# Second mixture's first half: all turned rows copied by ScalarE, gate logits ahead of the last quarter's v products, no memset behind its sends

## The chip, the cores and the metric

The kernel runs on one core of one Trainium2 chip, as one program. The time is the device time of that core in microseconds (us), from a launch to its end. The five engines are named as in the profile: PE is TensorE (its weight loads are PEld), DVE is VectorE, ACT is ScalarE, POOL is GpSimd, SP is SyncE, which here only issues DMAs. Each engine works through its own list of instructions in order. They meet through semaphores: a wait at the head of an engine's list holds back all that stands behind it.

## The reference

Two decoder layers on `x` of shape (2, 1024, 256), float32, with a layer norm behind each of six blocks. Only the last three matter here:

```python
x = _layernorm(x + _L1_attn_ref(x, ...), axis=-1)    # recurrent mix: k, v, r products, a scan over time
x = _layernorm(x + _L1_xattn_ref(x, ctx_1024, ctx_1024, ...), axis=-1)   # one head over 64 context rows
x = _layernorm(x + _L1_ffn_ref(x, ...), axis=-1)     # 16 experts and two shared ones

# in _L1_attn_ref, xt the normalised rows and x_prev the row before
K = einsum('btc,dc->btd', xt * mk + x_prev * (1.0 - mk), Wk)     # V and R alike, R through a sigmoid
S = scan(state * decay + k_t)
y = einsum('btc,dc->btd', R * ((S * first + K) * V), Wo)

# in _L1_ffn_ref
scores = jax.nn.sigmoid(x @ w_gate.T)                # 16 experts in 4 groups
top_groups = jax.lax.top_k(group_scores, 2)[1]       # two groups, then four experts of theirs
_, idx = jax.lax.top_k(masked, 4)
w = w / (w.sum(-1, keepdims=True) + 1e-06)
routed = einsum('tef,ehf,te->th', silu(x @ w1) * (x @ w3), w2_e, combine)
```

## The kernel before, in words

The 2048 rows are 16 tiles of 128 rows and stay in SBUF. The program is a chain of stages, each a block of its own on all engines: two attentions, the first mixture of experts, then `recurrent_stage` and `moe1_stage`. A stage begins on an engine when all engines have left the one before.

**The recurrent stage** does the recurrent mix and the second cross attention in four quarters of 512 rows. What each engine does, in which order, is one list of steps, `recurrent_plan`. Every engine goes through the whole list and does its part of each step. A step is (name, quarter, part): `k`, `v`, `r` are products of a quarter (two parts of 128 output columns each, L2229), `y` the output product (L2237), `x4` the norm behind it, `tx` turns (transposes) the normed rows, `s` makes the scores, `ta` turns the softmax's exponentials, `o` is the attention's result (L2285) and `x5` the norm behind it. For each norm, DVE takes the moments, POOL makes the reciprocal root in `spread_of` (L1979 to L1985), and DVE (x4) or ACT (x5) applies it.

Into the last quarter's steps the list already puts the first half of the routing for the second mixture, for rows 0 to 1023 (half 0):

- `tg` (L2266): PE turns the finished rows of quarters 0 and 1, four steps of four transposes. The result is copied from PSUM to `xTf`, parts 0 by ACT (L2064), parts 1 by DVE (L2182).
- `lg` (L2275): PE multiplies `xTf` by the gate's 16 columns. It first waits until all four turned parts are copied. ACT puts the exponential into `ex` (L2067).
- `c` parts 0 to 3: DVE picks groups and experts (`choose`, L2399 to L2433).
- `ct` (L2478): PE counts; `lc`: DVE works out each row's place (`locate`, L2441 to L2454), and sets `pos_ready`.
- `sx`: POOL sends rows to their places with `scatter`. One send is an indirect DMA of one tile of 128 rows (L2389); behind it stands `ch.pause`, a memset of 16 columns (L112) with a wait for it.

Half 0 has 8 tiles times 4 choices, 32 sends. Three are issued behind `pos_ready`, ten after step `y` of quarter 3, and the other 19 at the start of the next stage.

**The mixture stage** starts with the same work for half 1 (turn, logits L2823, choose, count, locate) and the shared experts (L2841, L2852). SP waits for all 32 sends of half 0, then loads the first sorted rows from `Xd` into `xin` (L2557). PE turns them (L2862), multiplies them with the experts' weights (L2879, L2891), item after item, 46 or so double tiles in a row. POOL sends half 1 meanwhile, two sends per item, each with its pause. At the end POOL gathers the results (L2601), and DVE adds, weighs and normalises.

PSUM banks of the recurrent stage are in two rings of four, `m` for k, v and r and `a` for the rest; a step waits until its bank's last use is drained.

Of the kernel before, what the change touches and what calls it, by code (L numbers as in the profile page):

```python
# [35 lines left out]
class Scope:  # L36
# [8 lines left out]
    def ps(self, name, shape, dt=F32):  # L45
        return self.stack.enter_context(self.nc.psum_tensor(f"{self.name}_{name}", shape, dt))

    def sem(self, name):
        s = self.stack.enter_context(self.nc.semaphore(f"{self.name}_{name}"))
        self.sems.append(s.num)  # L50
        return s
# [1788 lines left out]
def recurrent_plan():  # L1840


    plan = [("st", 0, 0), ("st", 1, 0), ("xn", 0, 0), ("tn", 0, 0), ("tn", 0, 1), ("df", 0, 0), ("mk", 0, 0), ("mv", 0, 0),
            ("mr", 0, 0), ("xn", 1, 0), ("kt", 0, 0), ("kt", 0, 1), ("km", 0, 0), ("km", 0, 1), ("bq", 0, 0)]
    for q in range(QUARTERS + 2):
        n, p, z = q + 1, q - 1, q - 2
        steps = [("x4", p, 0), ("x4", p, 1), ("k", q, 0), ("k", q, 1), ("x5", z, 0), ("x5", z, 1), ("tx", p, 0), ("tx", p, 1),
                 ("tn", n, 0), ("tn", n, 1), ("v", q, 0), ("v", q, 1), ("df", n, 0), ("s", p, 0), ("mk", n, 0), ("mv", n, 0),
                 ("r", q, 0), ("r", q, 1), ("ta", p, 0), ("dn", p, 0), ("rs", q, 0), ("rs", q, 1), ("st", q + 2, 0),
                 ("mr", n, 0), ("o", p, 0), ("o", p, 1), ("y", q, 0), ("y", q, 1), ("xn", q + 2, 0)]  # L1850
        plan += [x for x in steps if 0 <= x[1] < QUARTERS]

    def put(step, *new):
        at = plan.index(step) + 1
        plan[at:at] = new

    put(("tx", 2, 1), ("tg", 0, 0), ("tg", 0, 1), ("tg", 1, 0), ("tg", 1, 1))
    put(("v", 3, 1), ("lg", 0, 0), ("c", 0, 0), ("c", 0, 1), ("c", 0, 2), ("c", 0, 3))
    put(("r", 3, 0), ("ct", 0, 0))
    put(("r", 3, 1), ("lc", 0, 0), ("sx", 0, 3))  # L1860
    put(("y", 3, 1), ("sx", 3, 13))
    return plan
# [10 lines left out]
def recurrent_stage(nc, a, G, experts1, route):  # L1873
# [46 lines left out]
    R = ps("R", [P, 8, 512])  # L1920
# [4 lines left out]
    free = [sem(f"bank_free{n}") for n in range(8)]  # L1925
# [11 lines left out]
    def filled(eng, step):  # L1937

        bank, n = at[step]
        eng.wait_ge(ready[bank], n)  # L1940
# [18 lines left out]
    with nc.Block() as block:  # L1959

        @block.sync
        def _(sp):
            sp.dma_start(cols[:, :, :], a["rwkv_cols"]).then_inc(cols_in, 16)
            sp.dma_start(w[:, :, :, :], a["rwkv_w"]).then_inc(w_in, 16)
            for to, name in ((wkT, "xk1"), (ctxT, "ctxT"), (wq, "xq1"), (ctx, "ctx")):
                sp.dma_start(to[:, :, :], a[name]).then_inc(x_in, 16)
            sp.dma_start(bk[:, :], a["bk1"]).then_inc(x_in, 16)
            sp.dma_start(bq[:, :], a["bq1"]).then_inc(x_in, 16)
            sp.dma_start(m_i[:, :], a["mask1"].rearrange("b k -> (b k)").partition_broadcast(P)).then_inc(x_in, 16)
            experts1.prefetch(sp, a)  # L1970
# [46 lines left out]
        @block.scalar  # L2017
        def _(act):
            act.wait_ge(cols_in, 16)
            act.activation(decay[:, :], cols[:, 5, :], ACT.Sigmoid)  # L2020
            act.activation(first[:, :], cols[:, 6, :], ACT.Exp).then_inc(consts, 1)
            for what, q, k in PLAN:
                step, p = (what, q, k), q % 2
                if step in at.at:
                    bank, _n = at[step]
                if what == "xn":
                    act.wait_ge(rstd_ready[0], q + 1)
                    if q:
                        filled(act, ("tn", q - 1, 1))
                    for j in range(J):  # L2030
                        act.activation(xn[:, j, :], G.x_sb[:, q * J + j, :], ACT.Identity, bias=shift[0][p][:, j:j + 1],
                                       scale=rstd[0][p][:, j:j + 1]).then_inc(xn_ready, 1)
                if what == "tn":
                    filled(act, step)
                    act.activation(xt[:, k, column(q, 0)], R[:, bank, :], ACT.Identity,
                                   bias=cols[:, 1, k:k + 1], scale=cols[:, 0, k:k + 1]).then_inc(free[bank], 1)
                if what == "r":
                    filled(act, step)
                    if q:
                        act.wait_ge(rw_ready, KD * (q - 1) + k + 1)  # L2040
                    act.activation(sig[:, k, :], R[:, bank, :], ACT.Sigmoid).then_inc(free[bank], 1)
                if what == "kt":
                    filled(act, step)
                    act.activation(kT[:, k, :], R[:, bank, 0:K2], ACT.Identity, bias=bk[:, k:k + 1]).then_inc(free[bank], 1)
                if what == "tx":
                    filled(act, step)
                    if q:
                        filled(act, ("s", q - 1, 0))
                    act.activation(xT[:, 2 * k:2 * k + 2, :, :], R[:, bank, :].rearrange("p (t k c) -> p t k c", t=2, k=KD),
                                   ACT.Copy).then_inc(free[bank], 1)  # L2050
                if what == "s":
                    act.wait_ge(sub_ready, q + 1)
                    if q:
                        act.wait_ge(den_ready, q)
                        filled(act, ("ta", q - 1, 0))
                    act.activation(e[:, :, :], sub[:, :, :], ACT.Exp).then_inc(exp_done, 1)
                if what == "ta":
                    filled(act, step)
                    if q:
                        filled(act, ("o", q - 1, 1))  # L2060
                    act.activation(aT[:, :], R[0:SK, bank, :], ACT.Copy).then_inc(free[bank], 1)
                if what == "tg" and k == 0:
                    filled(act, step)
                    act.activation(route.xTf[:, k, 512 * q:512 * (q + 1)], R[:, bank, :], ACT.Copy).then_inc(free[bank], 1)  # L2064
                if what == "lg":
                    filled(act, step)
                    act.activation(route.ex[:, 0, :], R[:, bank, 0:route.CE], ACT.Exp, scale=-1.0).then_inc(free[bank], 1)  # L2067
                if what == "x5":
                    act.wait_ge(rstd_ready[2], 2 * q + k + 1)
                    for j in (2 * k, 2 * k + 1):  # L2070
                        last = act.activation(G.x_sb[:, q * J + j, :], xr[2][:, j, :], ACT.Identity,
                                              bias=shift[2][p][:, j:j + 1], scale=rstd[2][p][:, j:j + 1])
                    last.then_inc(x5_ready, 1)

        @block.vector
        def _(dve):
            ch = Chain(dve, c_dve)

            def moments(n, p, x_of, js):

                s = [ch.done(dve.bn_stats(st[n][p][:, j, :], x_of(j))) for j in js]
                for m, j in enumerate(js):
                    ch.wait(s[m])
                    last = dve.bn_aggr(mv[n][p][:, j, :], st[n][p][:, j, :])
                last.then_inc(var_ready[n], 1)

            for what, q, k in PLAN:
                step, p = (what, q, k), q % 2
                if step in at.at:
                    bank, _n = at[step]  # L2090
                if what == "st":
                    moments(0, p, lambda j: G.x_sb[:, q * J + j, :], range(J))
                if what in ("mk", "mv", "mr"):
                    n = ("mk", "mv", "mr").index(what)
# [18 lines left out]
                if what == "k" and k == KD - 1:  # L2113
# [10 lines left out]
                    for d in range(KD):  # L2124
                        ch.wait(scans[d])
                        bank = at[("k", q, d)][0]
# [41 lines left out]
                if what == "o":  # L2168
# [8 lines left out]
                    last.then_inc(free[bank], 1)  # L2177
                    drained(dve, step)
                    moments(2, p, lambda j: xr[2][:, j, :], (2 * k, 2 * k + 1))
                if what == "tg" and k == 1:  # L2180
                    filled(dve, step)
                    dve.tensor_copy(route.xTf[:, k, 512 * q:512 * (q + 1)], R[:, bank, :]).then_inc(free[bank], 1)  # L2182
                if what == "c":
                    if k == 0:
                        dve.wait_ge(route.consts, 1)
# [2 lines left out]
                if what == "lc":  # L2188
                    filled(dve, ("ct", 0, 0))
                    bank = at[("ct", 0, 0)][0]  # L2190
# [127 lines left out]
class Route1:  # L2318
# [64 lines left out]
    def scatter(self, pool, ch, G, Xd, n, lo, hi, rest):  # L2383

        pool.wait_ge(G.zeroed, 16)
        pool.wait_ge(self.pos_ready, n + 1)
        for m in range(lo, hi):
            s, r = m // self.W.K, m % self.W.K
            pool.indirect_dma_start(Xd[:, :], bass.IndirectOffsetOnAxis(self.pos[:, n, r, s:s + 1], 0),  # L2389
                                    G.x_sb[:, self.W.TH * n + s, :], None).then_inc(self.scattered[n], 16)  # L2390
            ch.pause(rest)

    def choose(self, dve, ch, n, part):

# [705 lines left out]
```

## Time and profile before

| what | us |
|---|---|
| median of 3 runs | 1311.39 (1308.12 to 1311.88) |
| the profiled execution | 1302.48 |
| its span | 1300.2 |
| PE busy | 1135.8 (87%) |
| DVE busy | 698.4 (54%) |
| ACT busy | 585.8 (45%) |
| POOL busy | 468.5 (36%) |

The profiled execution is a single one, 8.9 us shorter than the median of the runs. Its span leaves out 2.3 us around the program. The busy shares are averages over stages with different limits: the recurrent stage ends and the mixture stage starts at about 1063 us, and the part in question lies between 1010 and 1094 us, where no engine is busy throughout. PE's granted clock is given for each stretch as a share of the full 2.4 GHz; 0.50 is the other level, 1.2 GHz.

### The profile page before, as it was taken

How to read it: one execution, taken by the hardware profiler on the slowest of the kernel's cores; microseconds unless marked ns; L12 is line 12 of the kernel's file. 1: busy time of each engine (PE TensorE's matmuls, PEld its weight loads, DVE VectorE, ACT ScalarE, POOL GpSimd, SP SyncE). 2: the span in 40 equal slices, each digit the busy share in tenths (PEclk: the TensorE clock that was granted, in tenths of full speed). 3: DMA queues.
4: the chain of work that ended last, by engine and by line, in shares of the span. 5: the costliest groups of instructions: out<-in, count | busy, mean ns of one | idle time of the engine just before them, and what ended most of it. 6: DMA issues, size and time to landing. Idle time of an engine off the chain costs nothing. (4 is left out here: it accounts for less than half of the span.)

```text
span 1300.2 us, 23677 instructions
## 1 busy us (share of the span) xinstructions
PE 1135.8 (87%) x7485; PEld 826.0 (64%) x7526; DVE 698.4 (54%) x1886; ACT 585.8 (45%) x1071; POOL 468.5 (36%) x906
## 2 busy tenths in 40 slices
PE   7799898999877876999999999999598757999991
PEld 4344444444344543889999999988455545999961
DVE  4766666766344543622323232338589846555647
ACT  3267677677756643222323232332244222557720
POOL 7445332231422332013323232301323176716456
PEclk9699999999988997999999999999699858999996
DMA  9900200000000006501111111130520014867633
GB/s 349 359 2 9 91 1 1 1 1 1 2 1 1 1 1 216 243 17 34 41 34 41 34 39 36 38 124 19 183 95 1 13 62 140 259 194 237 216 105 122
DMA packets 68128, 109.31 MB, mean 84 GB/s; under 512 B 7346, under 2 KB 54963, under 8 KB 65203
## 3 DMA queue, kind: packets, MB, share of 16 engines
q1 hardware_dynamic: 58130, 80.96, 18.2%
q0 software_dynamic: 9888, 27.01, 6.5%
q8 instruction: 54, 0.88, 0.3%
q14 instruction: 56, 0.45, 0.1%
HBM read 65.61 MB, written 42.34 MB: 83 GB/s over the span
## 5 line engine op out<-in xcount | busy, mean ns | idle before, releaser
L1440 ACT ACTIVATE f_work<-f_bank,f_ub 128x128 f32<-128x128 f32 x312 | 89.0, 368 | 204.3 <-PE f_bank L1762 204.3
L512 ACT ACTIVATE att_PT<-att_RB 128x1024 f32<-128x1024 f32 (+1 forms) x192 | 147.8, 808 | 66.2 <-PE att_RB L651 35.0
L557 DVE CUSTOM_DVE_ANT_0 att_junk<-att_RB,att_causal_q 128x128 f32<-128x128 f32 (+3 forms) x256 | 120.6, 488 | 53.2 <-PE att_RB L633 43.9
L1762 PEld LDWEIGHTS f_bank<-f_work,f_xTf 128*128 128x128 f32 x1248 | 145.3, 192 | 3.9 <-DVE f_work L1562 2.0
L1762 PE MATMUL f_bank<-f_work,f_xTf 128*128 128x128 f32 x1248 | 145.9, 275 | 1.5 <-DVE f_work L1562 1.5
L1771 PE MATMUL f_bank<-wd_down,f_work 128*128 x624 | 141.2, 380 | 0.0
L633 PE MATMUL att_RB<-att_kT,att_qT 96*128 96x512 bf16 (+3 forms) x384 | 120.5, 350 | 20.4 <-DVE att_mx L557 6.8
L1771 PEld LDWEIGHTS f_bank<-wd_down,f_work 128*128 128x128 f32 x624 | 115.7, 190 | 13.9
L1391 POOL DMA_INDIRECT Yd<-f_work,f_inv x39 | 38.5, 987 | 196.3 <-DVE f_work L1581 196.3
L1571 DVE COPY f_xTf<-wu_up 128x1024 f32 x78 | 54.1, 695 | 102.6 <-PE f_bank L1762 94.9
L633 PEld LDWEIGHTS att_RB<-att_kT,att_qT 96*128 96x128 bf16 x384 | 34.4, 100 | 110.3 <-issue 39.1
L561 DVE TENSOR_REDUCE att_mx<-att_RB 128x1 f32<-128x512 f32 x128 | 88.1, 689 | 21.4 <-PE att_RB L633 21.1
L648 PE MATMUL att_RB<-att_qT,att_kT 128*128 128x512 bf16 (+3 forms) x353 | 94.6, 327 | 2.6 <-ACT att_PT L512 1.5
L2879 PEld LDWEIGHTS f_bank<-f_xT,f_staged 128*128 128x128 f32 x752 | 91.9, 193 | 2.6 <-DVE f_xT L2701 0.3
L2879 PE MATMUL f_bank<-f_xT,f_staged 128*128 128x128 f32 x752 | 92.3, 277 | 0.0
L2601 POOL DMA_INDIRECT f_ga<-Yd,r_pos x64 | 63.0, 984 | 72.3 <-DMA Yd<-f_yo 53.9
L2389 POOL DMA_INDIRECT Xd<-g_x,r_pos x64 | 64.2, 1003 | 52.7 <-DVE r_pos L2454 27.8
L663 PE MATMUL att_OT<-att_PT,att_vst 128*32 128x512 f32 (+3 forms) x768 | 82.5, 501 | 0.0
L1386 POOL DMA_INDIRECT f_work<-Xd,f_inv x39 | 50.4, 1293 | 77.8 <-PE f_bank L1737 66.2
L1581 DVE TENSOR_TENSOR f_work<-f_bank,f_db 128x256 f32<-128x256 f32 x39 | 16.6, 425 | 108.3 <-PE f_bank L1771 108.3
L384 POOL TENSOR_SCALAR att_negm<-att_rowmax 128x8 f32<-128x8 f32 x32 | 7.8, 245 | 179.6 <-DVE att_rowmax L565 179.6
L1726 PE MATMUL f_bank<-f_xTf,wu_up 128*128 128x256 f32 x256 | 57.1, 381 | 1.5 <-ACT f_work L1430 1.5
(462 smaller groups left out, 2150.9 us busy)
## 6 DMA issues: line engine op xcount, KB each, us to landing
Xd<-g_zero SPq DMA_DIRECT2D x1, 12032.0 KB, 40.7
f_xin<-Xd SPq DMA_DIRECT2D x47, 256.0 KB, 3.8
Yd<-f_yo SPq DMA_DIRECT2D x47, 256.0 KB, 2.8
wu_up<-up_w SPq DMA_DIRECT2D x9, 1024.0 KB, 9.0
wd_down<-down_w SPq DMA_DIRECT2D x9, 1024.0 KB, 18.4
w_all<-w SPq DMA_DIRECT2D x6, 768.0 KB, 10.6
wu_up<-Yd SPq DMA_DIRECT2D x16, 256.0 KB, 5.7
w_all<-w SPq DMA_DIRECT2D x1, 2304.0 KB, 17.2
```

What stands on the lines that cost most here:

```text
L512: act.activation(buf[:, :, 0:w], ST[:, 2 * (k % 2):2 * (k % 2) + 2, 0:w], ACT.Exp, scale=float(HD) ** -0.5).then_inc(exp_done, 1)
L557: dve.tensor_tensor_reduce(junk[:, k % RING, 0:w], RB[:, bank, 0:w], G.causal_q[:, 512 - w:512], 1.0, LOWEST, ALU.add, ALU.max, to).then_i ...
L561: dve.tensor_reduce(to, RB[:, bank, :], AX_X, ALU.max).then_inc(bank_free[bank], 1)
L633: pe.matmul(RB[:, bank, 0:w], qT[1 - p][0:MROW, r, t * P:(t + 1) * P], kT[1 - p][0:MROW, 512 * c:512 * c + w], start=True, stop=True).then ...
L648: mm = pe.matmul(to[:, 0:512 - off], kT[p][:, kt * P:(kt + 1) * P], qT[p][:, r, 512 * c + off:512 * c + 512], start=True, stop=not diag)
L663: mm = pe.matmul(OT[32 * r:32 * r + 32, off:512], vst[p][:, kt, :], PT[k % 4][:, h, 0:512 - off], start=(kt == 0), stop=(kt == 4 * c + 3))
L1440: last = act.activation(hT[:, u % 2, m, :], bank[:, UB + m // 4, (m % 4) * P:(m % 4 + 1) * P], ACT.Gelu, bias=ub[:, ds(e, 1), m])
L1762: mm = pe.matmul(bank[:, UB + n, P * m:P * (m + 1)], staged_up[:, kk, at:at + P], xT[:, u % 2, kk, :], start=(kk == 0), stop=(kk == KD - 1))
L1771: mm = pe.matmul(bank[:, YB + u % 2, 0:D], hT[:, u % 2, m, :], W.down[:, ds(e, 1), m, :].rearrange("p o c -> p (o c)"), start=(m == 0), st ...
L2389: pool.indirect_dma_start(Xd[:, :], bass.IndirectOffsetOnAxis(self.pos[:, n, r, s:s + 1], 0), G.x_sb[:, self.W.TH * n + s, :], None).then_ ...
L2601: pool.indirect_dma_start(ga[:, s, r, :], None, Yd[0:P * R * (n + 1), :], bass.IndirectOffsetOnAxis(pos[:, n, r, s:s + 1], 0)).then_inc(ga ...
L2879: mm = pe.matmul(bank[:, UB + p, P * at:P * (at + 1)], staged_up[:, q % 3, i, kk, F * part:F * (part + 1)], xT[:, p, i, kk, :], start=(kk ...
```

## The change

Three things are edited. The copies of all four turned parts are ACT's, DVE's two are gone. In the list of steps `lg` stands directly behind the last `tg`, ahead of the v products of quarter 3, where it stood behind them; DVE's `c` steps keep their place behind `v`. And for half 0 the pause behind each send is gone, in both stages; half 1 keeps it.

```diff
@@ recurrent_plan
-    put(("tx", 2, 1), ("tg", 0, 0), ("tg", 0, 1), ("tg", 1, 0), ("tg", 1, 1))
-    put(("v", 3, 1), ("lg", 0, 0), ("c", 0, 0), ("c", 0, 1), ("c", 0, 2), ("c", 0, 3))
+    put(("tx", 2, 1), ("tg", 0, 0), ("tg", 0, 1), ("tg", 1, 0), ("tg", 1, 1), ("lg", 0, 0))
+    put(("v", 3, 1), ("c", 0, 0), ("c", 0, 1), ("c", 0, 2), ("c", 0, 3))
@@ recurrent_stage, scalar
-                if what == "tg" and k == 0:
+                if what == "tg":
                     filled(act, step)
                     act.activation(route.xTf[:, k, 512 * q:512 * (q + 1)], R[:, bank, :], ACT.Copy).then_inc(free[bank], 1)
@@ recurrent_stage, vector
-                if what == "tg" and k == 1:
-                    filled(dve, step)
-                    dve.tensor_copy(route.xTf[:, k, 512 * q:512 * (q + 1)], R[:, bank, :]).then_inc(free[bank], 1)
@@ Route1.scatter
-            ch.pause(rest)
+            if n:
+                ch.pause(rest)
```

PE's list in the recurrent stage before, from the turned rows (`g_x` against the identity) to the counting of the chosen experts (`r_hot`); `rx_xm,rx_w` are the v and r products, `w_gate,r_xTf` the logits, `rx_km,rx_xT` the scores:

```order
L2266 MATMUL rx_R<-g_ident_f,g_x 128x128 x16
L2229 MATMUL rx_R<-rx_xm,rx_w 128x512 x4
L2275 MATMUL rx_R<-w_gate,r_xTf 128x16 x16
L2256 MATMUL rx_R<-rx_km,rx_xT 128x64 x8
L2229 MATMUL rx_R<-rx_xm,rx_w 128x512 x2
L2478 MATMUL rx_R<-r_hot,r_upper 128x128 x4
```

The same place of PE's list now (line numbers are three or two lower):

```order
L2263 MATMUL rx_R<-g_ident_f,g_x 128x128 x16
L2272 MATMUL rx_R<-w_gate,r_xTf 128x16 x16
L2226 MATMUL rx_R<-rx_xm,rx_w 128x512 x4
L2253 MATMUL rx_R<-rx_km,rx_xT 128x64 x8
L2226 MATMUL rx_R<-rx_xm,rx_w 128x512 x2
L2476 MATMUL rx_R<-r_hot,r_upper 128x128 x4
```

The 16 logit products and the four v products have changed places; nothing else on PE moved.

DVE's list at the same place before, from the scan of the last quarter to the first steps of the choice of experts:

```order
L2119 SCALAR_TENSOR_TENSOR rx_state<-rx_decay,rx_state,rx_R 128x512 x2
L2127 SCALAR_TENSOR_TENSOR rx_rw<-rx_state,rx_first,rx_R 128x512 x2
L2182 COPY r_xTf<-rx_R 128x512 x2
L2132 TENSOR_TENSOR rx_rw<-rx_rw,rx_R 128x512 x2
L2399 TENSOR_SCALAR r_ex<-r_ex 128x128
L2400 RECIPROCAL r_sg<-r_ex 128x128
```

DVE's list there now:

```order
L2119 SCALAR_TENSOR_TENSOR rx_state<-rx_decay,rx_state,rx_R 128x512 x2
L2127 SCALAR_TENSOR_TENSOR rx_rw<-rx_state,rx_first,rx_R 128x512 x2
L2132 TENSOR_TENSOR rx_rw<-rx_rw,rx_R 128x512 x2
L2397 TENSOR_SCALAR r_ex<-r_ex 128x128
L2398 RECIPROCAL r_sg<-r_ex 128x128
```

The two copies are gone. The two multiplications by v (`rx_rw<-rx_rw,rx_R`) still stand ahead of the choice (`r_ex`, `r_sg`).

POOL's list at the start of the mixture stage now, with the 19 sends left of half 0, the first one of half 1 in the same row, and then half 1's sends with their memsets:

```order
L2577 MEMSET f_half 128x4
L2386 DMA Xd<-g_x,r_pos 12032x256 x20
L112 MEMSET r_rest 128x16
L2386 DMA Xd<-g_x,r_pos 12032x256
L112 MEMSET r_rest 128x16
```

Before, each of the 20 sends had a memset row of its own behind it.

## Rows read from the trace of the kernel before

**Rows 1.** Chain that ended last, in order of time: start us, us, what.

```profile
1063.86 1.07 POOL Xd L2389
...
1089.03 2.45 DMA Xd<-g_x,r_pos
1091.49 2.79 DMA f_xin<-Xd
```

**Rows 2.** Waits of PE, 1000 to 1180: total us, times, longest.

```profile
PE f_bank L2862 <- DMA f_xin<-Xd: 7.7, 1, 7.7
```

**Rows 3.** Timeline of PE, 1010 to 1044: start us, us, [idle before].

```profile
1010.06 1.91 PE L2266 MATMUL rx_R<-g_ident_f,g_x 128*128 128x128 f32 x16
1011.81 3.60 PE L2229 MATMUL rx_R<-rx_xm,rx_w 128*128 128x512 f32 x8
1015.25 3.64 PE L2275 MATMUL rx_R<-w_gate,r_xTf 128*128 128x16 f32 x32
1018.74 3.29 PE L2256 MATMUL rx_R<-rx_km,rx_xT 128*128 128x64 f32 x16
1021.82 3.73 PE L2229 MATMUL rx_R<-rx_xm,rx_w 128*128 128x512 f32 x4
1027.87 0.38 PE L2478 MATMUL rx_R<-r_hot,r_upper 128*128 128x128 bf16 x4 [2.32 <-DVE r_hot L2433]
1028.32 1.94 PE L2229 MATMUL rx_R<-rx_xm,rx_w 128*128 128x512 f32 x4
1035.48 3.69 PE L2237 MATMUL rx_R<-rx_w,rx_rw 128*128 128x256 f32 x16 [1.08 <-DVE rx_rw L2136]
1043.77 2.17 PE L2244 MATMUL rx_R<-g_ident_f,g_x 128*128 128x128 f32 x8 [4.60 <-DVE g_x L2148]
```

**Rows 4.** Timeline of ACT at the turned rows.

```profile
1010.76 0.59 ACT L2064 ACTIVATE r_xTf<-rx_R 128x512 f32<-128x512 f32 x1
1011.57 0.60 ACT L2064 ACTIVATE r_xTf<-rx_R 128x512 f32<-128x512 f32 x1 [0.22 <-PE rx_R L2266]
```

**Rows 5.** Timeline of DVE, 1015 to 1059.

```profile
1015.45 0.69 DVE L2132 TENSOR_TENSOR rx_rw<-rx_rw,rx_R 128x512 f32<-128x512 f32 x1 [0.54 <-PE rx_R L2229]
1019.31 0.23 DVE L2399 TENSOR_SCALAR r_ex<-r_ex 128x128 f32<-128x128 f32 x1 [3.17 <-ACT r_ex L2067]
...
1040.39 0.66 DVE L2140 SCALAR_TENSOR_TENSOR rx_xr<-g_x,rx_R 128x512 f32<-128x512 f32 x1
...
1041.75 0.30 DVE L2084 BATCH_NORM_AGGREGATE rx_mv<-rx_st 128x2 f32<-128x6 f32 x2
...
1058.50 0.30 DVE L2084 BATCH_NORM_AGGREGATE rx_mv<-rx_st 128x2 f32<-128x6 f32 x2
```

**Rows 6.** Timeline of POOL, 1042 to 1060, at its norms.

```profile
1042.83 0.22 POOL L1979 TENSOR_SCALAR rx_rstd<-rx_mv 128x2 f32<-128x2 f32 x1
...
1059.26 0.23 POOL L1979 TENSOR_SCALAR rx_rstd<-rx_mv 128x2 f32<-128x2 f32 x1
```

**Rows 7.** Groups of POOL, 1063 to 1091: xcount, busy us, mean ns, idle before.

```profile
L2389 POOL DMA_INDIRECT Xd<-g_x,r_pos x19 | 18.9, 995 | 5.6 <-POOL r_rest L112 5.0 <-issue 0.7
L112 POOL MEMSET r_rest<- 128x16 f32 x19 | 2.4, 125 | 0.0
```

**Rows 8.** Groups of POOL, 1260 to 1291, gathers without a memset between them.

```profile
L2601 POOL DMA_INDIRECT f_ga<-Yd,r_pos x21 | 21.4, 1019 | 6.1 <-issue 6.1
```

**Rows 9.** Stretches: busy us of PE, PEld, DVE, ACT, POOL, then granted clock.

```profile
1019.00:1022.00 3.00, 3.00 (x17) 3.00 (x17) 2.49 (x10) 0.20 (x1) 0.00 (x0) 0.52 0.00 0
1022.00:1025.00 3.00, 3.00 (x5) 0.94 (x4) 2.72 (x17) 0.00 (x0) 0.00 (x0) 0.50 0.01 3
1043.50:1048.00 4.50, 4.23 (x19) 3.83 (x20) 0.92 (x3) 2.48 (x3) 3.75 (x7) 0.50 0.16 58
1067.00:1070.00 3.00, 2.33 (x21) 2.36 (x22) 2.63 (x5) 0.00 (x0) 2.44 (x5) 1.00 0.29 102
1070.50:1077.00 6.50, 6.50 (x15) 3.72 (x15) 5.56 (x20) 4.36 (x6) 5.11 (x11) 0.50 0.26 91
```

## The prediction, written before the result was known

> **What bounds the kernel now.** I read the chain that ended last first. It goes back only to 1063 us, to the start of the mixture stage, and its first members are POOL's sends of half 0: the first of 19 starts at 1063.86, the last at 1089.03, its rows land 2.45 us later, SP's load of the sorted rows takes 2.79 us, and only then, at 1094.42, PE turns them [rows 1]. The waits of PE say the same from the other side: 7.7 us for that load, the longest single wait of the stretch [rows 2]. From there PE works without a gap to about 1237, so what reaches 1094 earlier or later moves the end by as much, up to 7.7 us earlier. Ahead of 1063 the chain gives nothing, because the stage boundary cuts it, so I follow the recurrent stage by the engines' timelines. Its end is made by the last norm: POOL starts it at 1059.26, ACT applies it, and the next stage's POOL and PE start behind that. Back from there the links are score and attention of quarter 3, the turn at 1043.77, for which PE waited 4.60 us, the norm before it, the output product at 1035.48, and DVE, which from 1019.31 works nearly without pause through choice, place and norms [rows 3, 5, 6]. What started DVE at 1019.31 was the logits' exponential, 3.17 us of wait. So a shift of that start moves the whole tail of the stage, and the sends with it.
>
> **Logits ahead of v, and the copies.** Before, PE went from the turned rows straight into v at 1011.81, since v waits for nothing here [rows 3]. Now the logits are next, and they need all four copies. ACT began its two at 1010.76 and 1011.57, 0.6 us each, the second at once when PE had it ready [rows 4]; PE ends the fourth group of transposes near 1011.97 (1010.06 + 1.91). Four copies in a row on ACT, about half a us apart, end near 1012.8, and with about 0.15 us for the semaphore PE begins the logits at 1013.0. That is 1.2 us in which PE stands. The logits themselves take 3.44 + 0.05 us as before (1015.25 to 1018.74), v 3.60, so v's last product is done at 1013.0 + 3.5 + 3.6 = 1020.1. The exponential is ready at about 1016.9, 2.4 us earlier than before, but this is worth nothing: in DVE's order both multiplications by v stand ahead of the choice. Before, the second of them ran at 1015.45 and the choice waited for the exponential; now the choice waits for v, plus a multiplication of 0.69 (0.62 until the next may start) [rows 5]. It starts at 20.1 + 0.04 + 0.62 = 1020.75, against 1019.31: **1.4 us later**. The bounds are 0.9 (ACT's copies keep up with PE, 0.5 us less) and 1.9 (each of the added copies costs its full 0.6). The two copies taken from DVE gain nothing: they ran at a time when DVE would next have waited for v anyway, and DVE had 3.17 us to spare. Scores and r behind v on PE are pushed back too, and what hides them is DVE, which takes 8.4 us from the start of the choice to its last step while PE needs 6.
>
> **PE's clock under the v products.** This is the larger term. The granted clock was full up to 1019, and 0.52 and 0.50 in the two stretches from there, right behind the 32 logit products of 16 columns; it was back after the r product [rows 3, 9]. The same happened in the mixture stage: 1.00 from 1067 to 1070 while its logits began, 0.50 from 1070.5 to 1077 [rows 9]. Both times the fall to 1.2 GHz came during or just behind logits, and the lower level lasted about 6.7 us. Before, this fell on scores and one part of r, which DVE hides. Now it falls on v, for which DVE waits. Price from rows: four product records took 3.73 us at the lower level and 1.94 at the higher, in a row of eight 1.80 [rows 3]; so each record costs 0.48 more, and all eight 3.9. If the fall comes at the end of the logits, 5.5 to 6.5 us of lower level lie over v, six or seven records, 2.9 to 3.4 us. If it comes later, or the level is back earlier, half of it. I take **+3.0**, with 0 and 4.5 (all of v and the last of the logits) as ends.
>
> The Trainium skill, page "TensorE: Matmul & The Clock Gate", section "Part 1: The HAM clock gate", says that the gate goes by how busy the array has been of late and runs freely, not reset by the kernel. By that, the place of the fall differs from one execution to the next, and an execution in which it misses v would come out 3.0 us earlier than my sum. The trace agrees as far as it goes: two levels only, and two falls at logits, at different distances from their start.
>
> **POOL in the recurrent stage.** Three sends lose their pauses. A pause is 0.125 us of memset and 0.28 of wait (5.0 over 18), 0.405 together [rows 7]. Without one there is still a gap: 21 gathers without memsets had 6.1 us of "issue" before them, 0.30 each [rows 8]. So a send gains 0.105, not 0.405, except the last of a run, behind which a norm follows at once. Two gaps and one end: about 0.4 us. POOL came to the norm of `y` at 1042.83, when DVE's moments had been there since 1042.05 (1041.75 + 0.30) [rows 5, 6]; it was late by 0.8, so the 0.4 counts in full: **-0.4**. The ten sends behind it gain 1.1 us on POOL; the last norm started at 1059.26, DVE's moments were ready at 1058.80 (1058.50 + 0.30), and with POOL free it starts some 0.08 behind them: **-0.4**, and the other 0.7 is lost in waiting for DVE.
>
> **The 19 sends of the mixture stage.** They are on the chain. Removed: 18 pauses of 0.405, 7.3 us. Added: 18 gaps of 0.30, 5.4 us. **-1.9 us.** The ends: -7.3 if the sends close up entirely; and nothing, or half a us lost, if a send without pause is longer, as the gathers' 1019 ns stand to the sends' 995 [rows 7, 8]. I stay by the 0.30 because it is the gap of the same kind of instruction on the same engine. What is late next is not near: PE would wait until 1094.42 - 7.7 = 1086.7. Half 1's own sends keep their pauses and are paced by the items.
>
> **Sum.** 1.4 + 3.0 - 0.4 - 0.4 - 1.9 = +1.7 us. On the profiled execution, 1302.48, this gives 1304.2; its span goes from 1300.2 to 1301.9. The median of the runs is 8.9 us above that execution; the difference carries over, so the predicted time is 1311.4 + 1.7 = **1313.1**. What a measurement here can tell from no change is about 0.3%, 3.9 us, so this is "the same", on the slow side.
>
> **The rivals.** (a) PE's clock stays high through v, or the lower level is over before: 1.4 - 0.4 - 0.4 - 1.9 = -1.3, 1310.1. For it: the stretch of logits is only 3.5 us, and in this trace the level outlived it. Against: the 1 us of standing ahead of the logits is new. (b) Slower: the clock falls a second time, in the wait before the counting. With the choice 4.4 us later, counting starts near 1032.3 (1027.87 + 4.4), while scores and r, at the full level, end near 1026.7; PE stands over 5 us where it stood 2.32. Before, it stood 4.60 ahead of the turn at 1043.77, and the level was 0.50 behind it [rows 3, 9]. Then r's second part costs 1.8 more, the attention's output 1.8 by the same ratio, and y, 3.69 us, at least its first half, 1.8: 5.4. About 1.2 is hidden, since y was done at 1039.17 and DVE took its second half at 1040.39, and 0.8 by POOL's lateness and 0.4 by the rest: +3.0 above my sum, 1316.1. It decides from the point where PE's standing passes that of 1043.77. (c) Pauses are worth their full length: the 19 sends gain 7.3 instead of 1.9, sum 1.7 - 5.4 = -3.7, 1307.7. For it: the queue might accept the next send at once. Against: 0.30 stands before every gather of rows 8. (d) Nothing that is listed: a loss elsewhere, or the measurement.
>
> **How the numbers follow.** Forecast 0.40, (a) 0.27, (b) 0.20, (c) 0.05, rest 0.08. The likeliest is 1313.1, its own range 1311 to 1315 by the ends of the clock term. For 8 in 10 the range takes in (a) and (b) with the spread of the medians, 1308.1 to 1311.9 before: 1306 to 1317.5. Faster by over 0.3%, below 1307.5: most of (c), a little of (a) by spread, 0.10. Slower by over 0.3%, above 1315.3: 0.6 of (b), a little of the forecast, 0.18. The rest, 0.72, within.
>
> **What would show it.** In the changed trace: PE starts the logits 1 us or so behind the last transposes, at 1013; `r_ex` on ACT is early by over 2 us, and DVE's step on it is later than before, behind a wait for PE's v and not for ACT. The eight v records take 5 to 7 us together and the granted clock there is 0.5; if they take 3.6, (a) holds. Counting starts after 1029. The gaps between POOL's sends are "issue", 0.30. The last norm starts some 0.1 us behind DVE's moments. From the first of 19 sends to the last takes 23.3 us instead of 25.2. Wrong would be: gaps near zero, a choice that starts before 1019.3, or a wait of PE for the load that isn't the last gate before the experts.

## The result and the profile after

The changed kernel took 1319.53 us (median of 5 runs, 1318.57 to 1323.02), the kernel before beside it 1311.88 (1308.12 to 1312.32): ratio 1.006, 95% interval 1.0036 to 1.0083, 7.65 us slower. The prediction was 1313.1, in a range that ended at 1317.5. The profiled execution took 1318.57 us; its span, 1316.6, stands against 1300.2 of before. The profile's page begins so (busy us, share of the span, instructions):

```profile
span 1316.6 us, 23643 instructions
PE 1143.1 (87%) x7485; PEld 828.8 (63%) x7526; DVE 697.9 (53%) x1884; ACT 585.8 (44%) x1073; POOL 466.5 (35%) x874
```

The busy times of DVE, ACT and POOL are those of before within 2 us. PE's is 7.3 us longer, nearly all of it in four rows at its lower clock: the logits 0.7, v 2.8, the second part of r 1.4, and 1.9 in the shared experts' down products further down. The other 9 us of the longer span are standing time. First the recurrent stage, PE's timeline (start, us, engine, line, operation, count, idle before and its releaser); it answers to [rows 3]:

```profile
1009.10 1.91 PE L2263 MATMUL rx_R<-g_ident_f,g_x 128*128 128x128 f32 x16
1012.00 4.36 PE L2272 MATMUL rx_R<-w_gate,r_xTf 128*128 128x16 f32 x32 [0.99 <-ACT r_xTf L2064]
1016.19 6.41 PE L2226 MATMUL rx_R<-rx_xm,rx_w 128*128 128x512 f32 x8
1031.80 0.59 PE L2476 MATMUL rx_R<-r_hot,r_upper 128*128 128x128 bf16 x4 [5.69 <-DVE r_hot L2431]
1032.61 3.30 PE L2226 MATMUL rx_R<-rx_xm,rx_w 128*128 128x512 f32 x4
1039.44 3.69 PE L2234 MATMUL rx_R<-rx_w,rx_rw 128*128 128x256 f32 x16 [0.32 <-DVE rx_rw L2136]
1047.33 2.17 PE L2241 MATMUL rx_R<-g_ident_f,g_x 128*128 128x128 f32 x8 [4.20 <-DVE g_x L2148]
```

DVE there, with its two v multiplications and the choice behind them ([rows 5]), and the granted clock by stretches (seventh column from the stretch's length on; 1.00 is 2.4 GHz, 0.50 is 1.2; [rows 9]):

```profile
1019.99 0.69 DVE L2132 TENSOR_TENSOR rx_rw<-rx_rw,rx_R 128x512 f32<-128x512 f32 x1 [7.85 <-PE rx_R L2226]
1022.64 0.69 DVE L2132 TENSOR_TENSOR rx_rw<-rx_rw,rx_R 128x512 f32<-128x512 f32 x1 [1.97 <-PE rx_R L2226]
1023.25 0.22 DVE L2397 TENSOR_SCALAR r_ex<-r_ex 128x128 f32<-128x128 f32 x1
```

```profile
1012.00:1014.80 2.80, 2.80 (x26) 2.80 (x26) 0.14 (x1) 1.15 (x1) 0.00 (x0) 1.00 0.03 6
1014.90:1021.90 7.00, 7.00 (x15) 3.77 (x15) 0.69 (x1) 0.28 (x1) 0.00 (x0) 0.51 0.00 0
1028.90:1035.20 6.30, 3.40 (x11) 1.95 (x12) 5.92 (x34) 2.24 (x3) 0.00 (x0) 0.50 0.01 1
1035.40:1043.00 7.60, 6.47 (x30) 4.74 (x28) 7.43 (x23) 1.07 (x2) 3.95 (x6) 1.00 0.13 46
```

PE was at 2.4 GHz through the first logits, fell to 1.2 in their last part and stayed there through the v products, which took 6.41 us instead of 3.60. The choice of experts started 14.15 us behind the turns (1023.25 - 1009.10) instead of 9.25. "Behind the turns" counts from PE's first `tg` transpose here and below. The clock fell again in PE's wait before the counts, as rival (b) said, but was back before `y`, which took its 3.69 us as before. POOL's sends and the last norm ([rows 6, 7]):

```profile
1050.28 0.96 POOL L2386 DMA_INDIRECT Xd<-g_x,r_pos  x1 [0.30 <-issue]
1062.45 0.23 POOL L1979 TENSOR_SCALAR rx_rstd<-rx_mv 128x2 f32<-128x2 f32 x1 [0.29 <-DVE rx_mv L2084]
1067.04 1.07 POOL L2386 DMA_INDIRECT Xd<-g_x,r_pos  x1 [0.65 <-issue]
1090.76 0.96 POOL L2386 DMA_INDIRECT Xd<-g_x,r_pos  x1 [0.30 <-issue]
```

The gap is the forecast 0.30 of "issue", and the row of 19 takes 23.7 us from first to last start, where it took 25.17 [rows 1]. So far this trace explains about +4 - 1.5 us. What comes next was in no step of mine. The chain that ended last, then PE and DVE in the mixture stage ([rows 1, 2]):

```profile
1084.70 8.23 another core or an unknown queue
1092.97 5.59 PE f_bank L2850 x16
```

```profile
1092.97 5.59 PE L2850 MATMUL f_bank<-w_all,f_hs 128*128 128x256 f32 x16 [8.28 <-remote]
1098.85 1.04 PE L2860 MATMUL f_bank<-g_ident_f,f_xin 128*128 128x128 f32 x8
1105.57 3.78 PE L2877 MATMUL f_bank<-f_xT,f_staged 128*128 128x128 f32 x16 [5.68 <-DVE f_xT L2699]
```

```profile
1084.42 0.18 DVE L2426 FIND_INDEX8 r_ix<-r_top,r_ma 128x8 uint32<-128x16 f32 x1 [0.71 <-issue]
1086.55 0.18 DVE L2426 FIND_INDEX8 r_ix<-r_top,r_ma 128x8 uint32<-128x16 f32 x1 [1.17 <-issue]
1092.93 0.18 DVE L2429 CAST r_ixf<-r_ix 128x32 f32<-128x32 uint32 x1 [4.26 <-remote]
```

Before the shared experts' down products PE stood 8.28 us, and DVE stood too, in the middle of eight like instructions that wait for nothing, and once more for 4.26 us behind them, while POOL's sends ran on at 1.27 us each. "Remote" means that no recorded signal explains the release. Indeed records are missing: of the 4817 semaphore updates that this trace's instructions make, 174 have none; in the trace of before all 4849 are there. Of the landings of DMAs it has 3691 records, where another trace of the same program (e8 below) has 6022. Every instruction of DVE and POOL is recorded.

The shared experts' end was now PE's last gate: it turned the first gathered rows at 1098.85 with no wait for their load, which was 7.7 us in [rows 2]. The prediction had named such a thing as a sign of being wrong. Half 1's counts stood behind the down products on PE, so DVE, which works out half 1's places ahead of its copy of the turned rows, came late as well, and PE stood another 5.68 us before the first product with an expert's weights:

```profile
1099.05 0.42 DVE L2439 TENSOR_TENSOR_SCAN r_incl<-r_keep,f_bank 128x128 f32<-128x128 f32 x1 [4.20 <-PE f_bank L2476]
1104.84 1.28 DVE L2699 COPY f_xT<-f_bank 128x512 f32<-128x512 f32 x2
```

### The profile page after: what moved, and what is told of

Its sections match the earlier page's. It is cut to its first block and busy times, and to the rows that moved or that the text cites. A ratio compares the mean times of both kernels' runs of the same rounds, so it can differ in the third digit from the quotient of the medians.

```text
span 1316.6 us, 23643 instructions
## 1 busy us (share of the span) xinstructions
PE 1143.1 (87%) x7485; PEld 828.8 (63%) x7526; DVE 697.9 (53%) x1884; ACT 585.8 (44%) x1073; POOL 466.5 (35%) x874
```

## Experiments

Eighteen runs on five chips, each timed over 5 rounds against the kernel before on the same chip; results are ratios to it, with a 95% interval. The chips fall into two kinds. On chips 3 and 0 no trace lost an update, and the kernel before took 1302.2 us. On chips 2, 7 and 15 every trace (one a run) lost 155 to 183 updates of instructions, and it took 1312.1, 1308.6 and 1308.2. The run of record is of the second kind (1311.9 for the kernel before, 174 updates lost in the changed one's trace), the profile of before, at 1302.48, of the first. Below, "last send to turn" is the time from the start of the last of the 19 sends to PE's first turn of gathered rows (5.39 before, from 1089.03 to 1094.42), "loop" from there to the last down product of an expert (147.4 before), and the recurrent stage ends with ACT's last norm (51.8 behind the turns before).

### The parts of the change (chip 3)

e1, the order and the copies with all pauses kept:

```diff
-            if n:
-                ch.pause(rest)
+            ch.pause(rest)
```

> The changed order of steps and ACT's copies alone, every send with its pause. Theory A (order): v behind the logits, on a PE that has fallen to 1.2 GHz, makes DVE start the choice 3 to 5 us later than before; all of it reaches the end, as before the pauses gave back only 0.8 in this stage: 4 to 5 us above the kernel before, and no wait of several us in the shared experts of the mixture stage. Rival B (pauses): the whole loss of the changed kernel (7.7 us) comes from sends without pause; then this run is within 2 us of the kernel before. Rival C: the 8 us wait in the mixture stage comes from the new order, then it is here again.

Measured 1.0036 (1.0024 to 1.0047), +4.7 us. PE in its trace, logits and v:

```profile
1011.03 4.40 PE L2272 MATMUL rx_R<-w_gate,r_xTf 128*128 128x16 f32 x32 [0.99 <-ACT r_xTf L2064]
1015.26 6.37 PE L2226 MATMUL rx_R<-rx_xm,rx_w 128*128 128x512 f32 x8
```

No stand-still followed, and the stage's end moved by 4.96 us. That is theory A. So order plus clock is +4.4 forecast, +4.7 measured.

e2, the kernel before without half 0's pauses and nothing else:

```diff
-            ch.pause(rest)
+            if n:
+                ch.pause(rest)
```

> The pauses of half 0 alone are gone, order and copies as before. By my sum the sends would give 0.8 + 1.9 = 2.7 us. Theory B: sends without a pause between them hold up the other engines: several of them stop together for up to 8 us at the end of the 19 sends, and the run is 3 to 8 us slower than the kernel before in spite of the gain on POOL. Rival: that wait was the bad luck of one execution; then this run is 1 to 3 us faster than the kernel before.

Measured 0.9974 (0.9962 to 0.9986), -3.4 us by the ratio, -1.8 by the medians, around my -2.7. e3 and e4 are the kernel before and the changed kernel, unchanged.

> The kernel before, unchanged, for a second profile and for the spread: the same time within 0.3%. If waits of several engines together come by chance, this profile should have some as well, as its runs are 9 us above its first profile; if they come only with sends without pause, it has none and PE goes from one item to the next in 3.09 us throughout.

> The changed kernel, unchanged, for a second profile: 6 to 9 us above the kernel before. If the wait of 8.3 us ahead of the shared experts' second product belongs to the change, it is here again at the same place; if it is chance, it is elsewhere or gone. The gate's place should differ: with PE at 2.4 GHz through v the choice starts 1.4 us later than before, at 1.2 GHz 3 to 5.

e3: 0.9995 (0.9982 to 1.0007). e4: 1.0011 (0.9999 to 1.0023), +1.4 to +1.7 us: the prediction's sum, and not the 6 to 9 that I expected of e4 from the run of record. In e4's trace:

```profile
1008.07 3.72 PE L2272 MATMUL rx_R<-w_gate,r_xTf 128*128 128x16 f32 x32 [0.99 <-ACT r_xTf L2064]
1011.63 5.38 PE L2226 MATMUL rx_R<-rx_xm,rx_w 128*128 128x512 f32 x8
```

The same program spent 5.38 us on v here and 6.41 in the run of record, because the fall came and went at another place. That agrees with the rule of the Trainium skill, page "TensorE: Matmul & The Clock Gate", section "Part 1: The HAM clock gate", that the gate runs freely and is not reset by a kernel's start.

### Cures for the clock and the order (chip 0)

e5, the changed kernel with DVE's two last v multiplications behind the choice:

```diff
-                if what == "v":
-                    filled(dve, step)
-                    ...
+                if what == "v" and q < QUARTERS - 1:
+                    times_v(q, k)
@@ c, k == 3
+                        times_v(3, 0)
+                        times_v(3, 1)
```

> The changed kernel, with DVE's two multiplications by v of the last quarter moved behind the choice of experts. If the cost of the new order is that the choice waits for v (my step), the choice now starts about 2.5 us earlier than in the kernel before instead of 3 to 5 later; the two multiplications, 1.3 us, come onto DVE's path behind it, and the pauses' gain stays: 2 to 5 us faster than the kernel before. Rival: PE, not DVE, holds the stage at this place (counting stands behind scores and r on PE, which still ends near 1026); then most of it is lost and the run is within 1 us of the kernel before.

Measured 0.9986 (0.9977 to 0.9995), 3.9 us under the changed kernel (e8, on the same chip) and 1.8 under the kernel before, between the forecast's 2 to 5 and the rival's 1. The choice began 7.76 us behind the turns, but the clock then fell under `y`:

```profile
1025.02 0.39 PE L2483 MATMUL rx_R<-r_hot,r_upper 128*128 128x128 bf16 x4
1030.30 3.13 PE L2289 MATMUL rx_R<-rx_ctx,rx_aT 64*128 64x256 f32 x8 [2.27 <-ACT rx_aT L2061]
1033.36 5.88 PE L2241 MATMUL rx_R<-rx_w,rx_rw 128*128 128x256 f32 x16
```

e6, the changed kernel with logits four times as wide (ACT first copies the gate's 16 columns four times, and reads one of the four results for its exponential):

```diff
-                            mm = pe.matmul(R[:, bank, experts1.E * s:experts1.E * (s + 1)],
-                                           route.xTf[:, kk, s * P:(s + 1) * P], experts1.gate[:, kk, :],
+                            mm = pe.matmul(R[:, bank, 64 * s:64 * (s + 1)],
+                                           route.xTf[:, kk, s * P:(s + 1) * P], route.gate4[:, kk, :],
```

> The changed kernel, its 32 logit products 64 columns wide instead of 16 (the gate four times side by side, of which one copy is read), as many products at the same pace. If the fall of PE's clock under v is owed to what the array does in the logits, it stays at 2.4 GHz through v more often: v takes 3.6 us instead of 5.4 to 6.4, the choice starts 1.4 us later than in the kernel before, and the run is 1.5 to 3 us below the changed kernel. Rival: the standing still ahead of the logits makes the fall, or 64 columns are no different; then v is as slow as in the changed kernel and the time the same within 0.1%.

Measured 0.9986 (0.9978 to 0.9995), 3.7 us under the changed kernel for more columns of work:

```profile
1010.10 3.76 PE L2279 MATMUL rx_R<-r_gate,r_xTf 128*128 128x64 f32 x32 [0.99 <-ACT r_xTf L2069]
1013.69 3.65 PE L2233 MATMUL rx_R<-rx_xm,rx_w 128*128 128x512 f32 x8
```

The logits took 3.76 us instead of 4.36, v 3.65 instead of 6.41. The edit leaves the number and the order of PE's products alone, and PE stands the same 0.99 us ahead of the logits, so this standing alone doesn't make the clock fall. In the changed order v took 3.65 us in all four traces with wide logits (e6, e9, e17, e18), and 5.38 to 6.41 in all seven with narrow ones. The choice started 10.79 us behind the turns, 1.55 later than in the kernel before: that is the term of order and copies by itself, and the 3.36 from there to 14.15 is the clock's.

e7, the kernel before with all copies on ACT (`if what == "tg":`, DVE's two removed), and e8, the changed kernel for the third time:

> The kernel before with one edit, all four turned parts copied by ACT, the logits behind v as before and every pause kept. My step says nothing is gained or lost: DVE had 3.17 us of wait there and ACT is idle. Same time within 0.1%. Rival: the copies matter by themselves, by ACT's later table load or by DVE being free earlier; then 0.5 us or more either way.

> The changed kernel once more, unchanged: 1.7 us above the kernel before if the chip is as in the last runs (ratio 1.0011), 7 us above it if the chip is one on which the kernel before takes 1311 us. In the second case the profile should again show several engines standing still together, and records of semaphores missing.

e7: 0.9992 (0.9982 to 1.0003), no difference that can be told. e8: 1.0021 (1.0011 to 1.0031), +2.7 us; v 6.35 us, and its shared experts stand for nothing but the usual 0.86:

```profile
1084.96 3.72 PE L2850 MATMUL f_bank<-w_all,f_hs 128*128 128x256 f32 x16 [0.86 <-DVE f_hs L2679]
1095.39 1.94 PE L2860 MATMUL f_bank<-g_ident_f,f_xin 128*128 128x128 f32 x8 [6.27 <-DMA f_xin<-Xd]
```

### The run of record comes back (chip 2)

e9 is both cures together, e10 the kernel before without half 0's pauses and with wide logits, e11 the changed kernel, e12 the kernel of e2.

> The changed kernel with both cures together: 64 columns of logits a block (so that TensorE's clock stays at 2.4 GHz under the quarter's last v products, which took 3.65 us in that experiment instead of 6.35) and VectorE's two last v multiplications behind the choice. Theory (the stage's end is set by VectorE's start of the choice): logits from tg + 2.0, ended by + 5.8, exp by ScalarE, choice from about + 6.2 instead of + 9.24 before and + 14.15 in the changed kernel; each cure alone gave about -3.6 us against the changed kernel, both give -5 to -6.5: 1.2 to 3 us under either alone, ratio to the kernel before 0.9960 to 0.9980. Rival (TensorE takes over as the bound: it waits for the counts again, its clock falls in that wait, and the o and y products at 1.2 GHz eat what the choice gained, as they did with the choice alone put ahead): no better than either alone, ratio 0.9983 to 0.9990.

> The kernel before in its own order, without the pauses behind the first half's sends, and with logits 64 columns wide. With the pauses gone alone TensorE's clock fell once more under the y products of the last quarter (5.71 us instead of 3.69) and the time came to 0.9974 of the kernel before. Theory A (that fall follows the narrow logits too, and costs): the clock stays up, ratio 0.9960 to 0.9972. Theory B (in this order TensorE has room there, VectorE sets the end): the same as without the wide logits, ratio 0.9970 to 0.9980, y perhaps at 3.69 us with nothing gained.

> The changed kernel itself once more. If what I take for its steps' sum holds (the order +5, the pauses -3), it stands 1.5 to 3 us over the kernel before on the same chip, as in the two runs made so far here (ratios 1.0011 and 1.0021). If the +7.65 us of the run of record belong to the kernel on some chips, where several engines stood still together in the second mixture, such a chip shows them again: ratio 1.004 and more, with an idle time of over 5 us before the shared experts' down products; then the run with the pauses alone removed, beside it here, tells whether they are what calls it up (it would stand over the kernel before too).

> The kernel before with only the pauses behind the first half's sends removed, once more, as the mate of the changed kernel's run. If the pauses protect the engines in the second mixture from standing still while 32 sends land, this one shows ratio over 1.000 on a chip where the changed kernel shows 1.004 or more. If not, it repeats 0.996 to 0.9985.

Measured: e9 1.0019 (1.0004 to 1.0034), e10 1.0023 (1.0013 to 1.0033), e11 **1.0071** (1.0051 to 1.0092), e12 **1.0035** (1.0023 to 1.0048). e9 and e10 missed both of their theories, which knew nothing of the kinds of chip; e11 and e12 came out on the side where the pauses' removal costs. e12 is the same program as e2, which was at 0.9974: the pauses' removal gives 2 to 3 us on one chip and costs 4.6 on another. Its recurrent stage is e2's within 0.2 us (end 51.03 and 51.22 behind the turns); the loss begins here:

```profile
1079.80 0.59 PE L2842 MATMUL f_bank<-r_xTf,w_all 128*128 128x512 f32 x1
1088.45 5.47 PE L2853 MATMUL f_bank<-w_all,f_hs 128*128 128x256 f32 x16 [8.05 <-remote]
1100.93 3.78 PE L2880 MATMUL f_bank<-f_xT,f_staged 128*128 128x128 f32 x16 [5.68 <-DVE f_xT L2702]
```

The order's share is the same as on chip 3: 1.0071 - 1.0035 = 0.0036, as in e1.

### Which pauses, and is it they (chips 7 and 15)

e13 is the kernel before, e14 that of e1. e15 keeps the pauses behind the last 19 sends alone, e16 doubles those:

```diff
-            ch.pause(rest)
+            if n or m >= 13:
+                ch.pause(rest)
```

```diff
             ch.pause(rest)
+            if not n and m >= 13:
+                ch.pause(rest)
```

> The kernel before, unchanged, for its trace. On a chip where it takes 1312 us: the recurrent stage as in its other traces (stage end 51.8 us behind the turns), and the 10 us over its other traces' 1302 all in the second mixture: expert loop 157 to 160 us instead of 147.4, semaphore records missing; theory A (pauses protect the shared experts): no idle time over 2 us before the shared experts' down products, and the first turn of gathered rows 84.4 to 85.5 us behind the quarter's turns. Theory B (it stands still there as well): 87 us and more. On a chip where it takes 1302 us: the trace of before again.

> The order and ScalarE's copies alone, all pauses kept. Theory A (the pauses' removal is what costs on the chip that takes 1312 us): ratio 1.003 to 1.0045 on any chip, since the order's +5 us come from the recurrent stage. Theory B (the order's shift in time is what calls up the stand-stills): 1.006 and more on the chip that takes 1312 us, 1.0035 on others.

> The kernel before with pauses behind the last 19 sends of the first half alone, none behind its first 13. Theory A (the shared experts beside the last 19 sends are what has to be protected): on the chip that takes 1312 us ratio 0.9990 to 1.0005, no stand-still before the shared experts' down products; on others 0.9990 to 1.0000 (the 13 pauses are worth some 0.8 us of the 2.7). Theory B (the number of sends in flight from the start matters): 1.0015 to 1.0035 on the chip that takes 1312 us.

> The kernel before with the pauses behind the last 19 sends doubled: two blankings with their waits, by the trace 0.405 us in place of a gap of 0.30 for one, so about 0.24 to 0.4 us more for each of 19, 4.6 to 7.6 us later for the last send. Theory A (sends closer together than the machine can record and signal are what stops the engines): on the chip that takes 1312 us the time stays or falls (0.998 to 1.001), since fewer stand-stills pay for the later send; on others 1.003 to 1.006. Theory B (they have nothing to do with it): 1.003 to 1.006 everywhere.

Measured: e13 0.9999 (0.9989 to 1.0010), e14 1.0043 (1.0028 to 1.0058), e15 0.9994 (0.9984 to 1.0005), e16 1.0017 (1.0007 to 1.0026). The kernel before, with 183 updates lost, does not stand still in the shared experts:

```profile
1081.92 3.72 PE L2852 MATMUL f_bank<-w_all,f_hs 128*128 128x256 f32 x16 [1.04 <-DVE f_hs L2681]
1093.57 1.94 PE L2862 MATMUL f_bank<-g_ident_f,f_xin 128*128 128x128 f32 x8 [7.49 <-DMA f_xin<-Xd]
```

Its loop takes 153.6 us instead of 147.4 (157 to 160 was what I expected for a chip that takes 1312 us; this one takes 1308.6), and that is its whole 6 us over the profile that I predicted from. e14 and e15 fit theory A. Doubling the pauses bought no more: the last send came 3.4 us later, the time rose by 2.2, between the ranges of e16's two theories. No run on chip 7 is without the 19 pauses, so what their removal costs there isn't measured.

e17 is e9 with the last 19 pauses put back (the edit of e15), e18 is e9 again, on the same chip.

> The changed kernel with 64 columns of logits, VectorE's two last v multiplications behind the choice, and the pauses behind the last 19 sends put back (none behind the first 13). Theory A (these 19 pauses protect the shared experts where records are lost): last send to first turn 5.1 to 6 us on any chip; against the kernel before 0.9980 to 0.9995 everywhere, since the stage ends some 0.6 to 1 us earlier than before's and the rest is before's. Theory B (the stand-stills came from the chip and not from the pauses' absence): last send to first turn 8 us and more on a chip where records are lost, ratio 1.001 and more there.

> The same without the 19 pauses (none in the first half), on the same chip. Theory A: where records are lost it is 1.5 to 4 us over its mate with the pauses, with 8 us and more from the last send to the first turn and over 155 us of expert loop; where none are lost it is 1 to 2 us under its mate and 0.9970 to 0.9985 of the kernel before. Theory B: 1 to 2 us under its mate everywhere.

Measured: e17 0.9993 (0.9981 to 1.0005), e18 1.0003 (0.9985 to 1.0020). Their medians are alike, 1307.0 and 1306.9, so e18 isn't the 1.5 to 4 us slower that theory A asked for. Their spreads differ: e17's twelve executions lie between 1303.4 and 1309.1, e18's are eight from 1304.3 to 1307.6 and four from 1309.9 to 1314.0. The profiled one of e18, 1312.29 us, is of the upper group; first e17's, then e18's rows:

```profile
PEld f_bank L2876 <- issue: 7.5, 1, 7.5
PE f_bank L2876 <- DMA f_xin<-Xd: 7.4, 1, 7.4
```

```profile
PEld f_bank L2866 <- remote: 7.1, 1, 7.1
PE f_bank L2866 <- remote: 6.3, 1, 6.3
```

The waits of PE between 1060 and 1100 us (total, times, longest): with the pauses the longest is the known one for the load, without them the stand-still at the down products stands in its place. On chip 15 the profiled execution had the stand-still. That the eight short executions of e18 were without it is a guess from their times; they have no trace.

All traces, by last send to turn in us:

| | records lost | none lost |
|---|---|---|
| 19 pauses kept | e13 5.2, e14 5.2, e15 5.4, e16 5.9, e17 5.2 | before 5.4, e1 5.2, e3 5.4, e7 5.4 |
| none | changed 8.1, e9 9.2, e10 10.8, e11 10.5, e12 9.2, e18 8.4 | e2 5.5, e4 5.1, e5 5.3, e6 5.5, e8 5.1 |

Measured to PE's first product with an expert's weights, as in the changed kernel's trace above, the field at the lower left stands further apart: 14.8 to 17.6 us behind the last send, against 7.3 to 8.7 for pauses with records lost and 7.0 to 7.4 where none are lost. From that product to the last down product it takes 151.1 to 152.9 us with the 19 pauses and 151.6 to 155.0 without where records are lost, and 145.5 to 146.5 where none are. So what the missing pauses cost lies for the most part ahead of the first expert product (6.2 us of e18 against e17), and most of the longer loop behind it comes with the kind of chip, pauses or not.

## Why the prediction was wrong

- **Order and copies, +1.4.** Right: 1.55 in e6, where the clock stayed up. The 1.2 us of standing before the logits was 0.99.
- **Clock under v, +3.0.** Right: v took 2.8 us more, the logits' last part 0.7, and the choice started 3.36 later than in e6. e6 shows that it hangs on the narrow logits, e4 that it can be smaller. Together with the first term +4.7 to +5.6 (e1, e14) against 4.4.
- **Three and ten sends, -0.8.** Right in kind: gaps of 0.30, and the last norm just behind DVE's moments. The stage's end came 55.95 us behind the turns, 0.8 earlier than e1's 56.76.
- **Rival (b)** came in its first half only. The clock fell before the counts and r's part cost 1.4 us, but `y` ran at 2.4 GHz. I had put the fall's end too late.
- **The 19 sends, -1.9: the step that failed.** The size was right on chips that lose no records (1.5 us in the sends, -2.7 for all pauses by forecast, -1.8 to -3.4 by e2). On chip 2 the sign turned: +4.6 in e12, for all 32 pauses. Its ends, -7.3 and half a us lost, counted POOL's own time alone. I did not ask what a pause does for the other engines, nor list "pauses removed, others held up" as a rival with a price. Without the 19 pauses, in all six traces that lost records, PE stood 6.3 to 10.6 us before the shared experts' down products and 5.7 more before the first expert product; with them at most 1.1 and 1.6. That the pauses prevent this on one and the same chip rests on a single pair of traces, e17 and e18 on chip 15, whose medians are alike; chip 2, where the cost is measured, has no trace with pauses.
- **"The difference carries over": also wrong.** The 8.9 us between the profile and the median were no constant. The profile shows a kind of execution that loses no records; by their times, and by the changed kernel's trace, the timed runs were of the other kind. In e13, 6 us above the profile, the difference lies in the expert loop (+6.2); the rest of the 8.9 isn't located, as there is no trace of the kernel before from a chip on which it takes 1312 us.

By these parts the run of record adds up: order 1.0036 (e1, chip 3) and pauses 1.0035 (e12, chip 2) make 1.0071, 9.3 us, which e11 measured as one; the record's is 1.006 (1.0036 to 1.0083). Against e8, a trace of the same program, the profiled execution is 14.9 us longer: 0.6 before the turns, 7.7 by the first expert product (2.9 of them by the first turn of gathered rows), 6.4 from there to the last down product and 0.3 behind it.

What makes the engines stand is not shown. The load of the DMA engines alone isn't it: between 1084.7 and 1092.9 us they were busy for 0.31 of the time, as in e8, which didn't stand (0.29 from 1077 to 1086 us). Nor is there a sign of waiting for code: every one of the 336 DMA packets between 1084 and 1093 us is of the sends' queue, none of the queues that load instructions. The Trainium skill, page "NOTIFIC — the notification-queue block", section "7.1 Overflow: three behaviours, one of which stalls the engine", says that the path which writes the profile's records holds its producers back inside rather than lose a record, and can so throttle an engine; its section "4.1 Block-level registers (shared by all 10 queues)" says that the runtime clears this for the source of semaphore events. By that, such an overload would show as stand-stills with all instructions recorded and semaphore updates missing, which is what these traces have. No run shows the block itself, nor whether an execution without recording stands still. Open too is why the loop behind the first expert product is longer where records are lost: by 4.9 and 6.1 us with the pauses (e14 against e1, e13 against before), by 6.4 and 8.7 without (the changed kernel against e8, e12 against e2).

e2 (0.9974, chip 3), e5 and e6 (0.9986, chip 0) beat both kernels on their chips, and no kernel without the pauses does on chip 2. e17, meant for all, can't be told from the kernel before on chip 15.

## What to carry to other kernels

A pause between back-to-back DMAs of one engine may serve the others: before it goes, ask who signals and waits beside it, and price their standing. When a profile is 9 us under the median of the runs, find out what the profile lacks before adding a difference to either, and look at whether its records are complete. And if narrow products are followed by products on the path, try them wider: 64 columns cost 0.04 to 0.12 us more than 16 by themselves (3.68 and 3.76 against 3.64) and saved 2.8 us behind them.

## What was not expected of the hardware

- The same edit can gain on one chip and cost on another: 0.9974 on chip 3, 1.0035 on chip 2, both intervals clear of 1.
- With the logits ahead of v, 32 logit products of 64 columns took 3.76 us, and 16-column ones 3.72 to 4.44; only with the latter did the clock fall to 1.2 GHz under v (5.38 to 6.41 us against 3.65).
- An indirect send without a pause keeps 1.27 us of distance (0.96 and a gap of 0.30) even while PE and DVE stand still for 8 us.
